# A fused two-layer attention and mixture-of-experts kernel: VectorE's copies first, router rows turned in the projection, unread products in TensorE's waits, one power per row for two norms

## The chip, the cores and the metric

The kernel runs on one core of one Trainium2 chip. Its engines work side by side and meet through semaphores: TensorE (PE, with its weight loads as PEld), VectorE (DVE), ScalarE (ACT), GpSimd (POOL), and the queues of SyncE (SP) and POOL, which issue DMAs. The metric is the device time of one execution in microseconds (us); lower is better. Before the change it is 1354.61 us, the median of 3 runs (1350.93 to 1354.62).

## The reference, cut to what matters

There are four batches of 512 rows with 512 columns each, and a context of 128 columns per row. Four steps follow one another, and each adds to x:

```
x = x + attn0(layernorm(x), ctx)       # q = rms_norm(layernorm(x)), k = rms_norm(ctx), rotary, 16 heads
                                       # over 4 key groups, causal softmax, then @ w_out.T
x = x + ffn0(layernorm(x))             # gate/up/down with 1376 hidden columns, low-rank experts beside it
x = x + attn1(layernorm(x), ctx)       # similarity rows, layer norm over the keys, softmax: added to x
x = x + moe(layernorm(x))              # router of 64 experts, top 8, capacity 128, expert gate/up/down
```

`rms_norm(v) = v * rsqrt(mean(v*v) + 1e-5)`, `layernorm(v) = (v - mean) / sqrt(var + 1e-5)`. So a row of q goes through two norms: with variance v of the row, its scale is `(v + 1e-5)^-0.5 * (v / (v + 1e-5) + 1e-5)^-0.5`.

## The kernel before, in words

All orders are written out by hand, one program per engine. P = 128 rows are a tile, a batch has NT = 4 tiles (t = 0 to 3). The stages are: the start (`front_norms(0)` to `first_group(0)`), `attention(0)`, then for b = 0, 1, 2 the stage `ffn(b)` followed by `attention(b + 1)` with the *tail* of batch b woven into it, then `ffn(3)`, `last_tail(3)` with `last_list`, then 64 experts, and at the end a DMA that adds two halves of the output.

**The start.** VectorE takes statistics of context and x (`bn_stats`, `bn_aggr`, lines 1112 to 1138), GpSimd raises variances to the power -0.5 (`front_power`, line 606). One power takes the context's and x's first norm together; VectorE then works out the second variance (lines 1142 to 1144), and a second power gives the second norm. Line 1246 ends the scale and the shift, step 29 of a chain (`FIRST["scaled"]`); ScalarE's `query_rows` (line 810) waits for it. TensorE waits for all constants (`setup_loaded`) ahead of `first_group(0)`.

**Attention.** G = 4 groups (g) of four heads. For tile t TensorE makes scores (`scores`, six units: two of t = 3, two of t = 2, one of t = 1, one of t = 0), VectorE takes their maximum (`maximum(g, i)`, line 1344), ScalarE the exponentials (`exps`, line 850), TensorE transposes them (`turn`, line 1914), and VectorE or ScalarE copies them out of PSUM (`turned`, line 1353 or 863). The keys and queries of the next group are transposed as `stack` (line 1923) and copied out (lines 1358 and 868); GpSimd prepares them (`stacks`, lines 629 to 640). All transposes go through a ring of three PSUM banks in a written order (`turning_order`), so that each unit waits until the unit three places ahead has been copied out. `times_v(g)` (line 1933) ends a group; it needs all copies of the group. Then `normalise` (line 1377) multiplies by the turned inverse sums (`inverse`, line 1944).

**The tail of batch b, woven into attention(b + 1).** Group 0: x2 and its statistics (`stats_x2`), x2 transposed (`row_T`, line 1997), keys times rows (`keys_out`, line 1962). Group 1: variances and similarity rows (`spread`, `spread_rows`, `similarity`, VectorE's `y` and `peak`). Group 2: softmax's division and x3 (`divide_y`, `x3`, line 1319), statistics of x3 (`stats_x3`). Group 3: aggregation, power, `normed` (line 1274, the router's rows HN), and TensorE's `normed_T` (line 1954, "xT4"), four transposes a tile, in the ring between `turn(3, 2, 3)` and `turn(3, 0)`. Behind group 3 stand the context's transposes (line 2073), the output projection (`projected_out`), and `logits` (line 2005). In attention(0), without a tail, VectorE makes the next queries in two parts (`query_part`, two and three operations) between the copies.

**The last batch.** In `last_tail` nothing else runs beside the tail: similarity rows (line 2321), then VectorE and ScalarE work out x3 and HN, TensorE transposes HN (line 2334) and multiplies by the router (line 2339). `last_list` makes the experts' token lists: positions (line 2109), one-hot products (line 2120), the list itself (line 2157). Then the rows are gathered by DMA and the first expert starts (lines 2359 and 2369).

Of the kernel before, what the change touches and what calls it, by code (L numbers as in the profile page):

```python
# [94 lines left out]
def build(nc, x, ctx_in, w, out, hx, acc):  # L95
# [93 lines left out]
    fvar2, fscale, fms = sb("fvar2", [P, NT]), sb("fscale", [P, NT]), sb("fms", [P, NT])  # L189
# [129 lines left out]
    def bcast(ap, n):  # L319
# [26 lines left out]
    CONSTANTS = [(ident, w["ident"]), (identb, w["identb"]), (mask_qk, w["mask_qk"]),  # L346
                 (wk, w["wk"]), (low_rows, w["low_rows"]),
# [30 lines left out]
    LIST_PAIRS = (4, 8)  # L378
    FRONT_Q = (4, 5, 6, 8)
# [7 lines left out]
    def turning_order(tail):  # L387

        order = []
        for g in range(G):  # L390
# [24 lines left out]
            if tail and g == G - 1:  # L415
                order += [("xT4", 0, "a"), ("xT4", 1, "a")]
# [3 lines left out]
            if tail and g == G - 1:  # L420
                order += [("xT4", 2, "a"), ("xT4", 3, "a")]
# [56 lines left out]
    def ring(a):  # L478

        if a == 0:  # L480
            return Ring(ALONE, (4, 5, 7), 0, 0, 0, 0)
        return Ring(BESIDE, (7, 4, 5), a, len(ALONE) - len(BESIDE) + len(BESIDE) * a,
                    *(turned_by(ALONE, by) - turned_by(BESIDE, by) + turned_by(BESIDE, by) * a for by in "ad"))
# [13 lines left out]
    with nc.Block() as block:  # L497
        @block.sync
        def _(sp):
# [9 lines left out]
            for dst, src, n in ((wq_bc, w["wq"], C), (wkn_bc, w["wkn"], CKV)):  # L509
                sp.dma_start(dst[:, :], bcast(src, n)).then_inc(tables_loaded, 16)  # L510
            for dst, src in CONSTANTS:
                sp.dma_start(dst[(slice(None),) * len(src.shape)], src).then_inc(setup_loaded, 16)
# [85 lines left out]
        def _(pool):  # L598
# [7 lines left out]
            def front_power(fb, n):  # L606

                pool.wait_ge(S["f_in"], 1 + 2 * fb + n)
                if n == 1:
                    ins = pool.tensor_tensor(finv[:, :], fvar[:, :], mhalf[:, :], ALU.pow)  # L610
                else:
                    ins = pool.tensor_tensor(fms[:, :], fvar2[:, :], mhalf[:, 0:NT], ALU.pow)
# [194 lines left out]
        def _(act):  # L807
            def query_rows(t, c0, c1):

                act.activation(X[:, t, c0:c1], XIN[:, t, c0:c1], ACT.Identity, bias=fvar2[:, t:t + 1],  # L810
                               scale=fscale[:, t:t + 1]).then_inc(setup_act, 1)

            def first_stacks():

                act.wait_ge(S["f_dve"], FIRST["scaled"])
                for t in range(NT):
                    query_rows(t, 0, P)
                act.activation(KS[:, :, :].rearrange("p t (r s d) -> p t r s d", r=2, s=2)[:, :, :, 0, :].bitcast(F32R),
# [34 lines left out]
            def attention(a, turns, b):  # L853
# [33 lines left out]

                exps(a, 0, 0)
                exps(a, 0, 1)
                for g in range(G):  # L890
# [13 lines left out]
                    exps(a, g, 4)  # L904
                    if tail and g == 0:
                        normed_T("xT3", 2)
                    if tail and g == 2:
                        exp_y(3)
# [6 lines left out]
                    if tail and g == 3:  # L915
                        normed_T("xT4", 0)
                        normed_T("xT4", 1)
# [5 lines left out]
                    if tail and g == 3:  # L923
                        normed_T("xT4", 2)
                        normed_T("xT4", 3)
# [14 lines left out]
                act.wait_ge(S["o_ready"], 1 + G * (a + 1))  # L940
                act.activation(OTH[:, G - 1, :], OT[:, (G - 1) % 2, :], ACT.Copy).then_inc(S["oT_last_hi"], 1)
# [92 lines left out]
            def last_tail(b):  # L1034
# [10 lines left out]
                for t in range(NT):  # L1045
                    act.wait_ge(S["xT4_ps"], 1 + t + 1)
# [55 lines left out]
        def _(dve):  # L1102
# [9 lines left out]
            def front_norms(fb):  # L1112
# [4 lines left out]
                dve.wait_ge(S["x_loaded"], 16 * (fb + 1))  # L1117
                alone(dve, "dve")
                for i in range(2 * NT):
                    ins = dve.bn_stats(FST6[:, i, :], CTX[:, i, :] if i < NT else XIN[:, i - NT, :])  # L1120
# [5 lines left out]
                for i in range(2 * NT):  # L1126
                    alone(dve, "dve")
                    ins = dve.bn_aggr(FMV[:, i, :], FST6[:, i, :])
                    if i < 2 * NT - 1:
                        ins.then_inc(S["f_dve"], 1)  # L1130
                        fstep.n += 1
                    else:
                        fstep(ins)
                fstep(dve.tensor_tensor(fscale[:, :], FMV[:, 0:NT, 0], FMV[:, 0:NT, 0], ALU.mult))
                fstep(dve.tensor_tensor(fscale[:, :], fscale[:, :], FMV[:, 0:NT, 1], ALU.add))
                fstep(dve.tensor_scalar(fvar[:, 0:NT], fscale[:, :], EPS_RMS, None, ALU.add))
                sig(dve.tensor_scalar(fvar[:, NT:2 * NT], FMV[:, NT:2 * NT, 1], EPS_LN, None, ALU.add),
                    "f_in", 2 * fb + 1)

            def front_scales(fb, meanwhile=lambda: None):  # L1140
                dve.wait_ge(S["f_out"], 1 + 2 * fb + 1)
                fstep(dve.tensor_tensor(fscale[:, :], finv[:, NT:2 * NT], finv[:, NT:2 * NT], ALU.mult))
                fstep(dve.tensor_tensor(fscale[:, :], fscale[:, :], FMV[:, NT:2 * NT, 1], ALU.mult))
                sig(dve.tensor_scalar(fvar2[:, :], fscale[:, :], EPS_RMS, None, ALU.add), "f_in", 2 * fb + 2)
                meanwhile()
                dve.wait_ge(S["f_out"], 1 + 2 * fb + 2)
                fstep(dve.tensor_tensor(fscale[:, :], finv[:, NT:2 * NT], fms[:, :], ALU.mult))
# [96 lines left out]
            dve.wait_ge(tables_loaded, 16 * 6)  # L1244
            front_scales(0, lambda: fstep(first_keys(0, HD, [XN[:, 3, i * P:(i + 1) * P] for i in range(3)])))
            fstep(dve.scalar_tensor_tensor(out=fvar2[:, :], in0=FMV[:, NT:2 * NT, 0], scalar=-1.0, in1=fscale[:, :],
                                           op0=ALU.mult, op1=ALU.mult))
            assert fstep.n == FIRST["scaled"], fstep.n
            dve.wait_ge(setup_act, QUERY_ROWS)
# [77 lines left out]
            def attention(a, turns, b):  # L1327
# [81 lines left out]
                for g in range(G):  # L1409
# [7 lines left out]
                    if rows_in:  # L1417
                        n = stats_x2(b, 3)
# [1086 lines left out]
```

## Time and profile before

| what | us |
|---|---|
| median of 3 runs (lowest, highest) | 1354.61 (1350.93, 1354.62) |
| the profiled execution's own time | 1353.49 |
| its span in the trace | 1351.7 |
| mean granted TensorE clock, as a share of full | 0.957 |
| PE / DVE / ACT / POOL busy | 1199.0 / 746.7 / 525.7 / 447.2 |
| start, up to TensorE's first product | 20.67 |
| attention(0), first to last times_v | 46.35 to 94.97 |
| attention(1), first scores to its last times_v | 235.75 to 322.67 |
| last tail and list, up to the first expert's product | 929.24 to 997.87 |

The trace is of one execution. The engine table says how long each engine was busy; the chain of waits says who released whom on the way to the end; a table of stretches gives busy time and granted clock by stage. A granted clock of 1.00 is 2.4 GHz and 0.50 is 1.2 GHz.

### The profile page before, as it was taken

Reading aid. Unit: us, or ns where it says so; the run is one execution under the profiler, and the core shown is the slowest. Engines: PE = TensorE matmul, PEld = TensorE weight load, DVE = VectorE, ACT = ScalarE, POOL = GpSimd, SP = SyncE. Lnnn points to the kernel's source line nnn. Section 1 sums busy time; section 2 is a strip of 40 time slices with the busy share of each in tenths; the row PEclk is TensorE's granted clock in tenths of the full one; section 3 lists DMA queues with packets and bytes.
Section 4 is the critical chain, followed back from the end, with each engine's and each line's share of the span. In section 5 each row is a group of like instructions: output and inputs, shape, how many; then the busy total and the mean of one; then the engine's idle time right before and its main releaser. Section 6 shows DMA issues by size and latency. Waiting matters only on the chain.

```text
span 1351.7 us, 19376 instructions
## 1 busy us (share of the span) xinstructions
PE 1199.0 (89%) x6494; PEld 877.1 (65%) x6494; DVE 746.7 (55%) x1509; ACT 525.7 (39%) x1186; POOL 447.2 (33%) x506
## 2 busy tenths in 40 slices
PE   2789999888999988899999899998469999999990
PEld 2567787666777766777866677775346666666650
DVE  6866665785688678578866847563622222222220
ACT  4774222775412377442246643221223233333320
POOL 0531334321133532113443202121035655555530
PEclk9999999989999998999999899999569999999995
DMA  8012320001233000213300013624439999999847
GB/s 281 1 60 90 117 97 33 1 32 65 104 132 111 19 1 32 104 70 127 129 1 1 32 65 117 251 98 184 178 111 332 347 362 352 357 344 352 246 54 140
DMA packets 45745, 186.98 MB, mean 138 GB/s; under 512 B 6556, under 2 KB 9628, under 8 KB 31204
## 3 DMA queue, kind: packets, MB, share of 16 engines
q1 hardware_dynamic: 30804, 146.13, 28.3%
q0 software_dynamic: 14864, 39.85, 12.9%
q8 instruction: 44, 0.72, 0.2%
q14 instruction: 33, 0.27, 0.1%
HBM read 155.26 MB, written 34.90 MB: 141 GB/s over the span
## 4 chain that ended last, share of the span: by engine, by line
PE 71%; DVE 15%; ACT 4%; issue 3%; DMA 3%; POOL 2%; DVEq 0%; POOLq 0%; SPq 0%; ACTq 0%
PE PS L2369 13%; PE PS L1832 10%; PE PS L1834 9%; PE PS L1833 9%; PE PS L2385 4%; PE PS L1914 3%; PE PS L2389 3%; PE PS L1933 3%; DVE NM L1344 2%; PE PS L1851 2%; PE PS L2359 2%; ACT P L850 2%; DMA WRAW<-in_ffn 1%; DVE PT L1353 1%; PE PS L2202 1%
## 5 line engine op out<-in xcount | busy, mean ns | idle before, releaser
L2369 PE MATMUL PS<-WE,XGT 128*128 128x384 f32 x512 | 194.8, 504 | 1.5 <-DVE HM L1809 0.8
L850 ACT ACTIVATE P<-PS,NM 128x512 f32<-128x512 f32 (+3 forms) x256 | 132.0, 533 | 39.0 <-DVE NM L1344 38.6
L689 POOL CAST HH<-HID 128x512 fp32r<-128x512 f32 x44 | 37.2, 846 | 324.9 <-DVE HID L1697 320.6
L1832 PE MATMUL PS<-XTH,WHI 128*128 128x512 f32 x352 | 141.3, 401 | 3.4 <-DVE WLO L1640 3.4
L969 ACT ACTIVATE WHI<-WRAW 128x1280 fp32r<-128x1280 f32 x44 | 56.0, 1274 | 217.9 <-DMA WRAW<-in_ffn 217.9
L1834 PE MATMUL PS<-XTH,WLO 128*128 128x512 f32 x352 | 138.2, 393 | 0.0
L1833 PE MATMUL PS<-XTL,WHI 128*128 128x512 f32 x352 | 138.1, 392 | 0.0
L2369 PEld LDWEIGHTS PS<-WE,XGT 128*128 128x128 f32 x512 | 88.3, 192 | 57.7 <-issue 23.4
L1914 PE MATMUL PS<-ident,P 128*128 128x128 f32 x640 | 98.7, 291 | 28.2 <-ACT P L850 6.2
L1816 DVE COPY HMT<-PS 128x256 f32<-128x256 f32 x64 | 27.2, 425 | 163.7 <-PE PS L2378 163.7
L1344 DVE TENSOR_REDUCE NM<-PS 128x2 f32<-128x1024 f32 (+2 forms) x96 | 98.7, 1039 | 27.7 <-PE PS L1841 27.4
L1914 PEld LDWEIGHTS PS<-ident,P 128*128 128x128 f32 x640 | 74.9, 149 | 41.1 <-ACT P L850 19.9
L662 POOL TENSOR_TENSOR sm<-sm,mhalf 128x4 f32<-128x4 f32 (+1 forms) x20 | 17.7, 884 | 213.3 <-DVE sm L1263 187.4
L764 POOL DMA_INDIRECT XG<-hx,IDX x64 | 64.6, 1010 | 50.8 <-POOL IDX L761 39.8
L1078 ACT ACTIVATE SL<-PS 128x192 f32<-128x192 f32 x64 | 21.1, 330 | 154.6 <-PE PS L2369 154.6
L1832 PEld LDWEIGHTS PS<-XTH,WHI 128*128 128x128 f32 x352 | 66.3, 188 | 20.3 <-DVE WLO L1640 6.2
L1834 PEld LDWEIGHTS PS<-XTH,WLO 128*128 128x128 f32 x352 | 66.3, 188 | 16.1
L1833 PEld LDWEIGHTS PS<-XTL,WHI 128*128 128x128 f32 x352 | 66.3, 188 | 14.1
L1353 DVE COPY PT<-PS 128x512 f32<-128x512 f32 (+1 forms) x96 | 61.4, 639 | 16.7 <-PE PS L1914 16.6
L1851 PE MATMUL PS<-KST,QST 128*128 128x512 f32 (+3 forms) x256 | 67.0, 366 | 2.7 <-ACT P L850 2.2
L776 POOL DMA_INDIRECT out<-YE,IDX x32 | 51.0, 1593 | 53.4 <-ACT YE L1084 36.5
L2385 PE MATMUL PS<-WE,HMT 128*128 128x256 f32 x256 | 66.0, 381 | 0.5 <-DVE HMT L1816 0.5
(312 smaller groups left out, 2702.2 us busy)
## 6 DMA issues: line engine op xcount, KB each, us to landing
WE<-in_we SPq DMA_DIRECT2D x64, 1152.0 KB, 8.0
WRAW<-in_ffn SPq DMA_DIRECT2D x44, 1060.0 KB, 4.9
acc<-HN SPq DMA_DIRECT2D x17, 256.0 KB, 6.0
XIN<-in_x SPq DMA_DIRECT2D x4, 1024.0 KB, 5.8
out<-X SPq DMA_DIRECT2D x4, 1024.0 KB, 4.2
out<-acc POOLq DMA_DIRECT2D x1, 4096.0 KB, 22.9
hx<-HN SPq DMA_DIRECT2D x3, 1152.0 KB, 4.5
CTX<-in_ctx SPq DMA_DIRECT2D x4, 256.0 KB, 2.8
```

Source lines behind the costliest of these rows:

```text
L764: pool.indirect_dma_start(out=XG[s][:, :], out_offset=None, in_=hx, in_offset=bass.IndirectOffsetOnAxis(ap=IDX1[s][:, 0:1], axis=0),).then ...
L850: act.activation(prob(t, n), PS[:, c0:c0 + (t + 1) * P], ACT.Exp, bias=NM[:, c:c + 1], accum_out=SSUM[:, c:c + 1]).then_inc(S["p_ready"], 1)
L969: act.activation(WHI[slot][:, 0:WD], WRAW[slot][:, 0:WD], ACT.Copy).then_inc(S["wg_hi"], 1)
L1344: dve.tensor_reduce(NM[:, t * HPG + n0:t * HPG + n0 + nh], src, AX, ALU.max, negate=True).then_inc(S["s_max"], 1)
L1353: dve.tensor_copy(prob_T(t, n0, nh), src).then_inc(S["ring_d"], 1)
L1832: pe.matmul(dst, a[0], b_[0], start=first, stop=False, **kw)
L1833: pe.matmul(dst, a[0], b_[1], start=False, stop=False, **kw)
L1834: return pe.matmul(dst, a[1], b_[0], start=False, stop=last, **kw)
L1851: pe.matmul(PS[:, a:a + n_keys], QST[n0 + n][:, t * P:(t + 1) * P], KST[:, 0:n_keys], start=(a % 512 == 0), stop=False, skip_group_check=True)
L1914: mm = pe.transpose(bank(bk, c, c + P), prob(t, n0 + n)[:, j * P:(j + 1) * P], ident[:, :])
L2369: mm = pe.matmul(bank(2 + s % 2, 0, 2 * F1), XGT[s % 2][:, k, :], WE[s][:, k * 2 * F1:(k + 1) * 2 * F1], start=(k == 0), stop=(k == KC - 1))
L2385: pe.matmul(bank(5 + h, 0, CH), HMT[s % 2][:, 0, :], WE[s][:, EDOWN + h * CH:EDOWN + (h + 1) * CH], start=True, stop=False)
```

## The change

There are five edits.

1. *VectorE's copies first.* In the woven attention VectorE's tail work moves behind `maximum` and `turned`; in attention(0) each `query_part` moves behind a copy. Instructions stay the same. ScalarE copies `xT3` tile 2 out ahead of `exps(4)`.
2. *Router rows turned in the projection.* `normed_T` leaves the ring; its four tiles are transposed between the parts of `projected_out`, into banks 6, 7, 1, 6, and ScalarE copies them out there, with semaphores of their own. The context's transposes move ahead of `times_v(3)`. The ring starts at another bank.
3. *Unread products.* `keep_clock(bank, n)` issues n products of 512 columns (bf16) into a bank that nobody reads: 10 at the start, 54 ahead of the transposes of HN in the last tail, 14 and 18 in `last_list`, 22 behind it.
4. *One power for both norms.* x's scale becomes `(v * (1 + 1e-5) + 1e-10)^-0.5`, one power of 4 columns; the context's power is a second one of 4 columns. The statistics of the context no longer wait for x.
5. *Loads.* ident, identb and mask_qk count towards `tables_loaded`; TensorE waits at the start for that only, and for `setup_loaded` ahead of the first projection.

```
+    ROWS_BANK = (6, 7, 1, 6)
-        return Ring(BESIDE, (7, 4, 5), a, ...
+        return Ring(BESIDE, (4, 5, 7), a, ...
 # front_norms: x waited for only at i == NT; x's aggregation first
+                        sig(dve.tensor_scalar(fvar[:, NT:2 * NT], FMV[:, NT:2 * NT, 1], 1.0 + EPS_RMS,
+                                              EPS_LN * EPS_RMS, ALU.mult, ALU.add), "f_in", 2 * fb + 1)
-                fstep(dve.tensor_tensor(fscale[:, :], finv[:, NT:2 * NT], finv[:, NT:2 * NT], ALU.mult))
-                fstep(dve.tensor_tensor(fscale[:, :], fscale[:, :], FMV[:, NT:2 * NT, 1], ALU.mult))
-                sig(dve.tensor_scalar(fvar2[:, :], fscale[:, :], EPS_RMS, None, ALU.add), "f_in", 2 * fb + 2)
 # VectorE, one group g of attention after the change (tail work in brackets, by group)
     maximum(g, 2); turned(g, 3, 0); query_part(1, 1) if g == 0
     [1: weighted] [2: y(3)]
     maximum(g, 3); turned(g, 3, 2)
     [2: peak(3)] [1: similarity_variances] [3: stats_x3(1)]
     normalise(g - 1); maximum(g, 4); turned(g, 2, 0)
     [1: similarity_scales, y(0)]
     maximum(g, 5); stack(g + 1, 1)
     [0: stats_x2(3)] [1: peak(0)]
     turned(g, 2, 2); query_part(g + 2, 0)
     [0: stats_x2(0)] [1: y(1)] [2: divide_y(0, 2), x3(0)] [3: stats_x3(2)]
     stack(g + 1, 3); turned(g, 1, 0, 2)
     [0: stats_x2(1)] [1: peak(1)] [2: x3(1)]
     divisors(g)
     [3: stats_x3(3), aggregate, variances]
     turned(g, 0, 0, 4)
     [3: normed, all four tiles]
     maximum(g + 1, 0); maximum(g + 1, 1); query_part(g + 2, 1)
     [0: stats_x2(2), aggregate, variances] [1: y(2), peak(2)]
     [2: divide_y(2, 4), x3(2), x3(3), stats_x3(0)]
 # TensorE
+            def keep_clock(bk, n):
+                for _ in range(n):
+                    pe.matmul(bank(bk).rearrange("p (r k) -> p r k", k=P), identb[:, :],
+                              mask_qk[:, :].unsqueeze(1).broadcast_to([P, NT, P]), start=True, stop=True)
+                    if g == G - 1:
+                        context_T()
                     times_v(g)
                 for t in range(NT - 1):
                     if t == 1:
                         inverse(G - 1)
                     projected_out(t, 0, KC - 1)
+                    if tail and t < 2:
+                        normed_T(2 * t)
+                        normed_T(2 * t + 1)
 # ScalarE, behind group 3: unload(3); xT4 tiles 0, 1; output_high(); xT4 tiles 2, 3
```

## Rows read from the trace of the kernel before

**Rows 1.** Page: busy us (share) xinstructions; chain of waits by engine; one costly group.
```profile
PE 1199.0 (89%) x6494; PEld 877.1 (65%) x6494; DVE 746.7 (55%) x1509; ACT 525.7 (39%) x1186; POOL 447.2 (33%) x506
...
PE 71%; DVE 15%; ACT 4%; issue 3%; DMA 3%; POOL 2%; DVEq 0%; POOLq 0%; SPq 0%; ACTq 0%
...
L2369 PE MATMUL PS<-WE,XGT 128*128 128x384 f32 x512 | 194.8, 504 | 1.5 <-DVE HM L1809 0.8
```

**Rows 2.** Stretches, one per attention group: length, PE PEld DVE ACT POOL busy, clock, DMA.
```profile
46.35:63.68 17.33, 14.45 (x125) 10.49 (x124) 14.93 (x23) 13.62 (x42) 7.48 (x13) 1.00 0.00 1
63.68:79.38 15.70, 14.29 (x126) 10.53 (x124) 12.11 (x18) 13.82 (x42) 8.55 (x11) 1.00 0.01 1
79.38:92.68 13.30, 11.00 (x97) 7.62 (x96) 10.24 (x15) 11.97 (x39) 6.46 (x3) 1.00 0.00 1
235.70:257.06 21.36, 17.48 (x124) 13.25 (x122) 17.15 (x30) 16.65 (x46) 7.86 (x14) 1.00 0.00 1
257.06:280.45 23.39, 21.64 (x150) 14.25 (x148) 16.75 (x28) 15.30 (x47) 9.69 (x16) 1.00 0.00 1
280.45:301.19 20.74, 17.40 (x126) 13.42 (x125) 18.07 (x29) 14.29 (x45) 5.52 (x7) 0.84 0.14 51
301.19:320.37 19.18, 14.40 (x113) 10.85 (x112) 14.24 (x26) 13.73 (x42) 2.84 (x3) 0.91 0.01 1
```

**Rows 3.** Chain of waits, then instructions in time, at the start: start us, us, what.
```profile
7.28 3.26 DVE FST L1120 x8
...
10.68 1.07 DVE L1128 BATCH_NORM_AGGREGATE FMV<-FST 128x2 f32<-128x6 f32 x8 [0.15 <-DVE FST L1120]
12.64 1.68 POOL L610 TENSOR_TENSOR finv<-fvar,mhalf 128x8 f32<-128x8 f32 x1 [12.21 <-DVE fvar L1137]
15.05 0.29 DVE L1200 TENSOR_TENSOR XN<-CTX,finv 128x128 f32<-128x128 f32 x1
17.02 1.65 ACT L810 ACTIVATE X<-XIN,fvar,fscale 128x128 f32<-128x128 f32 x4 [15.00 <-DVE fvar L1246]
20.67 1.08 PE L1868 MATMUL PS<-ident,KS 128*128 128x128 f32 x4 [20.67 <-DVE KS L1232]
```

**Rows 4.** Instructions in time in attention(0), with the idle time before them.
```profile
43.83 0.40 POOL L629 CAST KS<-KR 128x256 fp32r<-128x256 f32 x1 [2.94 <-DVE QR L1226]
54.46 0.60 PE L1923 MATMUL PS<-ident,KS 128*128 128x128 f32 x4
61.88 0.63 PE L1914 MATMUL PS<-ident,P 128*128 128x128 f32 x4 [1.49 <-DVE PT L1353]
92.68 2.36 PE L1933 MATMUL PS<-PT,CTX 128*32 128x512 f32 x32 [0.83 <-issue]
```

**Rows 5.** The same in attention(1).
```profile
245.63 0.63 PE L1997 MATMUL PS<-ident,X 128*128 128x128 f32 x4 [2.18 <-DVE PT L1353]
288.77 1.77 DVE L1319 SCALAR_TENSOR_TENSOR X<-XN,sm,X 128x512 f32<-128x512 f32 x2
292.28 1.09 PE L1923 MATMUL PS<-ident,QS 128*128 128x128 f32 x4 [1.85 <-DVE PT L1353]
```

**Rows 6.** A stretch of the last tail, columns as in rows 2.
```profile
947.50:958.00 10.50, 0.00 (x0) 0.00 (x0) 8.60 (x20) 2.33 (x6) 1.01 (x1) 0.50 0.92 372
```

**Rows 7.** TensorE's instructions in time: two of attention(1), then the last tail.
```profile
248.29 0.39 PE L1841 MATMUL PS<-mask_qk,identb 128*128 128x512 bf16 x1
336.05 3.68 PE L2005 MATMUL PS<-rw,XTF 128*128 128x64 f32 x32
...
958.42 3.67 PE L2334 MATMUL PS<-ident,HN 128*128 128x128 f32 x16 [14.19 <-DVE HN L1274]
961.89 6.93 PE L2339 MATMUL PS<-rw,XTF 128*128 128x64 f32 x32
986.54 3.65 PE L2157 MATMUL PS<-OWN,SPREAD 128*128 128x64 f32 x16 [1.20 <-DVE OWN L1589]
997.87 4.90 PE L2369 MATMUL PS<-WE,XGT 128*128 128x384 f32 x8 [0.73 <-issue]
```

More of the change, by code:

```diff
@@ L939, in attention @@
                 unload(G - 1)
-                act.wait_ge(S["o_ready"], 1 + G * (a + 1))
-                act.activation(OTH[:, G - 1, :], OT[:, (G - 1) % 2, :], ACT.Copy).then_inc(S["oT_last_hi"], 1)
+                if tail:
+                    for t in range(NT):
+                        act.wait_ge(S["xT4_ps"], 1 + NT * b + t + 1)
+                        act.activation(XTF[:, :, t * P:(t + 1) * P], bank(ROWS_BANK[t]).rearrange(
+                            "p (k q) -> p k q", k=KC), ACT.Copy).then_inc(S["xT4_sb"], 1)
+                        if t == 1:
+                            output_high()
+                else:
+                    output_high()
             def softmax_exp(b):
@@ L1859, in ranks_out, with keep_clock @@
                       skip_group_check=True).then_inc(S["ffn_ps"], 1)
+            def keep_clock(bk, n):
+                for _ in range(n):
+                    pe.matmul(bank(bk).rearrange("p (r k) -> p r k", k=P), identb[:, :],
+                              mask_qk[:, :].unsqueeze(1).broadcast_to([P, NT, P]), start=True, stop=True)
             def first_group(fb):
@@ L2000, in logits @@
                 def logits():
[L2002 removed]
+                    pe.wait_ge(S["xT4_sb"], 1 + NT * (b + 1))
                     for t in range(NT):
@@ L2007, in logits, with context_T @@
                     mm.then_inc(S["lgt_ps"], 1)
+                def context_T():
+                    for t in range(NT):
+                        mm = pe.transpose(bank(0, t * P, (t + 1) * P), CTX[:, t, :], ident[:, :])
+                    mm.then_inc(S["ctxT_ps"], 1)
                 for g in range(G):
@@ L2053, in attention @@
                     turn(g, 1, 2, 2)
-                    if tail and g == G - 1:
-                        normed_T("xT4", "xn4_ready", HN, 2)
-                        normed_T("xT4", "xn4_ready", HN, 3)
                     if g < G - 1:
@@ L2069, in attention @@
                         keys_out()
-                if tail:
-                    turns.out(pe, "xT4", NT - 1)
-                for t in range(NT):
-                    mm = pe.transpose(bank(0, t * P, (t + 1) * P), CTX[:, t, :], ident[:, :])
-                mm.then_inc(S["ctxT_ps"], 1)
                 def projected_out(t, k0, k1):
@@ L2089, in attention @@
                     projected_out(t, 0, KC - 1)
+                    if tail and t < 2:
+                        normed_T(2 * t)
+                        normed_T(2 * t + 1)
                 pe.wait_ge(S["ctxT_sb"], 1 + a + 1)
```

218 lines of the change are left out of this document (110 added, 108 removed).

## The prediction

> **What bounds the kernel now.** I read the page first: TensorE is busy for 1199.0 of 1351.7 us, and it holds 71% of the chain that ended last, VectorE 15% [rows 1]. So time can be won only where TensorE waits or runs at a low clock. The table of stretches says where that is. In the groups of attention(1) TensorE is busy for 17.48 of 21.36, 21.64 of 23.39, 17.40 of 20.74 and 14.40 of 19.18 us, and in the last two the mean granted clock is 0.84 and 0.91, which means 1.2 GHz for about 6.6 and 3.5 us (share below 1.00, doubled, times the length) [rows 2]. Attention(2) and (3) repeat these stretches within 0.1 us from group 1 on. Third, the instructions in time name what TensorE waits for: VectorE's copies. Fourth, the last tail: 14.19 us without a product, and 1.2 GHz from then on until the first expert [rows 6, 7]. The feed-forward stages (TensorE busy throughout) and the 64 experts are not touched, so whatever comes earlier ahead of them moves the end by as much.
>
> **The start (one power, loads).** Before, eight statistics take 3.26 us from 7.28 on, behind x's arrival [rows 3]. The context's four are a quarter as wide; the x rows take about 0.6 us each, so x's end at about 9.75. Half of the eight aggregations (1.07) is 0.54, one variance operation 0.2: GpSimd starts at 10.7. Its power took 1.68 for 8 columns [rows 3]; for 4 I take 1.1, which lies between nothing and 1.68. One shift operation later, at 12.1, ScalarE may scale rows; before it was 17.02: 4.9 us earlier. The keys need the second power too: it starts at 12.0 (context's aggregation and three operations stand ahead), ends at 13.1, and the key work, begun at 15.05 before, begins at 13.2, now all of it ahead of the query's first operations. Keys 1.6, first query 1.3, low part 0.4: TensorE's first transposes at about 16.5 instead of 20.67 [rows 3]. I take 4.1 (bounds: 1.8, what the keys' start moves by, and 4.9). The wait for tables costs nothing if they land by 13 us; they are about 2 MB, and what was loaded up to then is more. The 10 unread products end before 16.5 even at twice 0.39 each. The first four transposes took 1.08 against 0.60 later [rows 3, 4], so the start runs slowly; I count nothing for that.
>
> **Attention(0), copies first.** In groups 0 and 1 the query's three operations stand ahead of the copy that TensorE waits for: 1.49 us in each (one of the two is shown) [rows 4]. Group 2, without them, takes 15.70 against group 1's 17.33 [rows 2]. That is 1.5 us twice, 3.0. GpSimd gets the queries about 5 us later (it started at 43.83 [rows 4], for some 6.5 us of stacks), while TensorE asks for their first stack at 54.46 [rows 4]; moved 1.5 earlier that is 53.0, and the stack is ready by about 51. So nothing is lost; without that cover it would be the 5 us. The context's transposes (0.44) fall into the 0.83 us in which TensorE waits ahead of the last times_v [rows 4]: 0.4. Sum 3.4 (bounds 0 and 3.7).
>
> **Attention(1) to (3), copies first and rows moved.** I walked each group through its ring.
> Group 0: `row_T(1)` waited 2.18 us for a copy that stood behind three statistics [rows 5]. With maximum and copy first that copy is 1.7 us earlier; ScalarE's early copy of tile 2 saves as much again in part, and the statistics fill VectorE's waits. Of the 3.9 us not busy [rows 2] I take 2.1. Group 0's last statistics and the aggregation (1.2 us) stand ahead of GpSimd's power and so of its stacks, which start some 5 us later; TensorE has `keys_out` (3.2 us) and a third of a group ahead of them, so nothing.
> Group 1: 1.75 us not busy; `y(0)` ahead of `maximum(5)` and the copy ahead of `peak(1)` remove two waits of 0.86 and 0.56: 1.3.
> Group 2: two x3 (1.77) and a reciprocal stand ahead of `maximum(4)`, and TensorE stands still for 1.85 until the copy, then runs its transposes at half rate (four in 1.09) [rows 5]. After the change VectorE is about 1.9 us earlier at `maximum(4)` and 2.5 at `maximum(5)`; then ScalarE (exponentials, `exp_y(3)` ahead of the stack's copy) is late next, and TensorE waits for it for about 1.8 us instead of 1.0. Of 3.3 us not busy and 3.3 lost to the clock I take 2.8.
> Group 3: attention(0)'s group 3, without a tail, takes 13.30 [rows 2]. The tail's remains: VectorE enters 1.3 us late from x3 and statistics behind group 2, and the last statistic with aggregation (1.2) stands ahead of the last copy. 13.3 + 1.3 + 1.2 = 15.8, against 19.18: 3.3 (bounds: 0 and 5.9).
> The projection grows by 16 transposes at 0.11 each (32 small products take 3.68 [rows 7]): 1.8, less 0.4 for the context's, which move into the wait ahead of times_v: 1.3 in the order of the engines, since TensorE has no gap there. ScalarE's copies are done 1 us before TensorE asks for the context's.
> Sum: 2.1 + 1.3 + 2.8 + 3.3 - 1.3 = 8.2 a batch, 24.6 for three (bounds -1.3 and 13 a batch).
>
> **The last tail.** 54 products follow line 2321 at about 944. The nearest row has one at 0.39 with its latency [rows 7]; behind one another I take 0.23, the spacing of the 512-column products of the same trace: 12.4 us, inside the gap of 14.19. (Price of one between 0.2 and 0.39; at 0.39 they would end 7 us late.) Then the clock should be up at 958.4. Transposes and logits took 3.67 and 6.9; at full rate 1.9 (VectorE paces HN) and 3.7 as in attention(1) [rows 7]: 5.1 saved. The 14 and 18 products (3.2 and 4.1) stand in waits of 4.8 and 5.0 us less one fold product: nothing. The one-hot products are few per us, so whether the clock holds until line 2157 (3.65, half of it to win) is even: 1.2 with the last one-hots. The 22 behind it take 5.1 in a wait of 5.8; if at half rate at first they are up to 2 us late, and then the first expert's 8 products cost 3.0 (194.8/512 each [rows 1]) instead of 4.90. I take 1.2 net. Sum 7.5 (bounds -8, if all run at half rate, and 10.5).
>
> The Trainium skill ("TensorE: Matmul & The Clock Gate", Part 4: PE-mode transpose) says that transposes don't count as busy for the clock. That speaks against the 5.1 above, since 16 transposes follow the 54 products; the 16 and the 32 logits here ran wholly at half rate [rows 7], which agrees. By it the tail would gain 3 rather than 7.5.
>
> **Sum.** 4.1 + 3.4 + 24.6 + 7.5 = 39.6. The profiled execution took 1353.5, so 1313.9; the median of the runs is 1.1 above that execution: 1315.
>
> **Rivals.**
> (a) *ScalarE takes VectorE's place.* It is busy for 60 us of 84.7 in the four groups of attention(1), 16.65 of 21.36 in group 0 [rows 2], and its order hardly changes. Then TensorE's idle time is renamed and the clock still falls in groups 2 and 3: 4 us a batch instead of 8.2, and 2 less elsewhere: 39.6 - 12.6 - 2 = 25, so 1330. For it: both stalls of group 2 end near a ScalarE copy. Against it: the largest waits end with VectorE's copies.
> (b) *The clock is down at HN.* Between the last of 54 and the first transpose 2 us stay open; a wait of 1.85 was enough for half rate at 292.28 [rows 5]. Logits stay slow, later products run at half rate, the tail gains 3: 1319.5.
> (c) *The moved work is paid in full.* What VectorE did inside a group now stands right ahead of `maximum(g+1, 2)` and of the last copy: 1.2 behind group 0, 2.1 behind group 2, 1.2 in group 3, with the projection 1.3, that is 5.8 a batch, 17.4, and 1.45 twice in attention(0), while the earlier copies win nothing. Less 4.1 and 7.5 that is 8.7 slower: 1363. It decides if VectorE's idle time ahead of that maximum (1.2 us in attention(0), as in group 3) is shorter than the moved work and TensorE waits for exponentials anyway. Against it: the wait of 2.18 at 245.63 [rows 5].
> (d) *The slow clock in the products themselves*, 108 of them at twice 0.23 against 28 us of waits: 20 us late in the tail, with the rest as forecast 1342.
>
> **How the numbers follow.** Forecast 0.54, (b) 0.18, (a) 0.18, (d) 0.04, (c) 0.04, no change 0.02. The forecast's own range is 1303 to 1327. 8 in 10 reach from 1302 to 1335, which takes in (a) and (b) and leaves (c) and (d) out. A measurement of this kernel tells 0.3% (4 us) from nothing. Faster 0.94, the same 0.02, slower 0.04.
>
> **What would show it.** TensorE's first transposes at 16.5; group 2 of attention(1) near 18 us with a clock of 0.95 or more, group 3 near 16; the projection's first part 1.3 longer; 54 products ending ahead of HN; logits in 3.7 us. The forecast is wrong if the groups stay above 20 and 18 us, if TensorE waits for ScalarE's exponentials for as long as it did for copies, if a product of 512 columns costs near 0.39, or if logits still take 6.9.

## The result, and the profile after

The changed kernel takes **1322.37 us**, median of four runs (1322.07 to 1322.65), beside 1353.69 for the kernel before on the same chip: ratio **0.977**, 95% interval 0.975 to 0.979, a gain of 31.3 us. I had said 1315, with 1302 to 1335 as the range: the sign held, and so did the mechanism in the groups and at the start; the size was 7 to 8 us too large. A second session gave 1322.28 for the same kernel. All medians here are of fast executions; one of e8's six took 2425.51 us and is not counted. The profiled execution took 1322.24 us with a span of 1320.4 (before: 1353.49 and 1351.7).

The page: busy us of each engine, then the chain of waits by engine, then a costly group.

```profile
PE 1214.4 (92%) x6612; PEld 874.8 (66%) x6612; DVE 744.1 (56%) x1493; ACT 525.3 (40%) x1186; POOL 442.0 (33%) x506
...
PE 71%; DVE 14%; ACT 6%; issue 3%; DMA 2%; POOL 2%; DVEq 0%; SPq 0%; POOLq 0%; ACTq 0%
...
L2388 PE MATMUL PS<-WE,XGT 128*128 128x384 f32 x512 | 192.7, 499 | 1.5 <-DVE HM L1813 0.8
```

Against [rows 1] TensorE is busy for 15.4 us more in a span that is 31.3 shorter (the 118 unread products alone are 29.8 us of it, the rest is shorter by 14.4); VectorE's share of the chain fell by a point and ScalarE's rose by two. The stretches, from one times_v to the next (columns as in [rows 2]): attention(0) groups 1 to 3, attention(1) groups 0 to 3 and from times_v(3) to the logits; then the stretch to the logits in attention(2) and in attention(3).

```profile
40.59:56.43 15.84, 14.29 (x125) 10.48 (x123) 15.30 (x23) 13.79 (x42) 7.70 (x12) 1.00 0.00 1
56.43:72.34 15.91, 14.20 (x125) 10.52 (x124) 13.68 (x21) 14.18 (x42) 10.48 (x14) 1.00 0.00 1
72.34:85.93 13.59, 11.51 (x99) 8.22 (x100) 10.59 (x15) 11.71 (x39) 6.47 (x3) 1.00 0.01 2
228.52:248.17 19.65, 17.39 (x123) 13.22 (x122) 15.61 (x24) 16.45 (x46) 5.43 (x10) 1.00 0.01 1
248.17:271.06 22.89, 22.05 (x148) 14.39 (x148) 18.19 (x33) 15.25 (x46) 11.44 (x18) 1.00 0.01 1
271.06:288.83 17.77, 15.02 (x126) 10.87 (x126) 15.02 (x25) 14.29 (x45) 5.29 (x9) 1.00 0.01 1
288.83:304.64 15.81, 12.31 (x100) 8.91 (x100) 14.74 (x27) 11.42 (x38) 0.75 (x1) 0.92 0.18 68
304.64:323.69 19.05, 19.05 (x107) 13.57 (x107) 8.44 (x16) 6.80 (x13) 2.80 (x4) 0.89 0.30 115
...
531.42:549.71 18.29, 18.29 (x106) 13.26 (x107) 8.40 (x16) 6.80 (x13) 2.79 (x4) 0.92 0.32 120
...
757.46:774.45 16.99, 16.99 (x106) 13.08 (x107) 8.45 (x16) 6.80 (x13) 2.81 (x4) 1.00 0.33 129
```

Group 2 fell from 20.74 to 17.77 and its clock rose from 0.84 to 1.00; group 3 from 19.18 to 15.81. But the same instructions from times_v(3) to the logits take 19.05, 18.29 and 16.99 us, and the clock column says why: 0.89, 0.92, 1.00. Before they took 15.68 in all three, without the 16 transposes of the rows. TensorE's instructions in time show the place, and the tail:

```profile
16.36 1.11 PE L1878 MATMUL PS<-ident,KS 128*128 128x128 f32 x4 [2.24 <-DVE KS L1235]
...
302.26 1.09 PE L1924 MATMUL PS<-ident,P 128*128 128x128 f32 x4 [1.22 <-ACT PT L863]
303.14 1.06 PE L2025 MATMUL PS<-ident,CTX 128*128 128x128 f32 x4
304.64 4.44 PE L1943 MATMUL PS<-PT,CTX 128*32 128x512 f32 x32 [0.44 <-issue]
...
918.45 11.82 PE L1868 MATMUL PS<-mask_qk,identb 128*128 128x512 bf16 x54
932.81 3.07 PE L2352 MATMUL PS<-ident,HN 128*128 128x128 f32 x16 [2.54 <-DVE HN L1280]
935.67 4.29 PE L2357 MATMUL PS<-rw,XTF 128*128 128x64 f32 x32
...
958.04 3.65 PE L2173 MATMUL PS<-OWN,SPREAD 128*128 128x64 f32 x16 [1.20 <-DVE OWN L1593]
961.48 6.29 PE L1868 MATMUL PS<-mask_qk,identb 128*128 128x512 bf16 x22
...
968.93 2.82 PE L2388 MATMUL PS<-WE,XGT 128*128 128x384 f32 x8 [0.73 <-issue]
```

times_v(3) takes 4.44 us instead of 2.36: it runs at 1.2 GHz for nearly all of it. In the tail the spread (OWN, SPREAD) is still at half rate, the first expert's eight products no longer (2.82 against 4.90 in [rows 7]). Last, TensorE's waits in total (us, times, longest):

```profile
PE PS L1924 <- ACT KST L868: 11.7, 9, 1.7
...
PE PS L1924 <- ACT PT L863: 7.2, 10, 1.2
PE PS L1924 <- ACT P L850: 6.2, 13, 0.8
```

The waits for VectorE's copies, up to 2.18 us each in [rows 5], are 0.4 us at most now; the large ones that are left inside attention end with ScalarE.

### The profile page after: what moved, and what is told of

Same layout as the page of the kernel before. It is cut to its first block, busy times and chain, and to the rows that moved or that the text cites. A ratio compares the mean times of both kernels' runs of the same rounds, so it can differ in the third digit from the quotient of the medians.

```text
span 1320.4 us, 19584 instructions
## 1 busy us (share of the span) xinstructions
PE 1214.4 (92%) x6612; PEld 874.8 (66%) x6612; DVE 744.1 (56%) x1493; ACT 525.3 (40%) x1186; POOL 442.0 (33%) x506
## 4 chain that ended last, share of the span: by engine, by line
PE 71%; DVE 14%; ACT 6%; issue 3%; DMA 2%; POOL 2%; DVEq 0%; SPq 0%; POOLq 0%; ACTq 0%
PE PS L2388 13%; PE PS L1836 10%; PE PS L1838 9%; PE PS L1837 9%; PE PS L2404 4%; ACT P L850 4%; PE PS L2408 3%; PE PS L1924 3%; DVE NM L1350 3%; PE PS L1943 2%; PE PS L2378 2%; PE PS L1855 2%; DMA WRAW<-in_ffn 2%; PE PS L2219 1%; PE PS L2218 1%
## 5 line engine op out<-in xcount | busy, mean ns | idle before, releaser
L1924 PE MATMUL PS<-ident,P 128*128 128x128 f32 x640 | 94.5, 280 | 25.8 <-ACT KST L868 11.7
L1924 PEld LDWEIGHTS PS<-ident,P 128*128 128x128 f32 x640 | 69.9, 142 | 40.3 <-ACT P L850 24.6
L692 POOL TENSOR_TENSOR HL<-HID,HH 128x512 fp32r<-128x512 f32 x44 | 64.6, 1468 | 3.5
## 6 DMA issues: line engine op xcount, KB each, us to landing
out<-acc POOLq DMA_DIRECT2D x1, 4096.0 KB, 22.9
```

Of the source, the lines that this page charges most:

```text
L692: pool.tensor_tensor(HL[slot][:, :], HID[:, :], HH[slot][:, :], ALU.subtract).then_inc(S["hl_ready"], 1)
L1924: mm = pe.transpose(bank(bk, c, c + P), prob(t, n0 + n)[:, j * P:(j + 1) * P], ident[:, :])
```

## The experiments

Each was timed beside the kernel before, whose median was 1353.79 us for e1 to e4, 1354.19 for e5 to e8, 1354.12 for e9 and e10, and 1354.26 for e11 and e12; these are four sessions on four chips. A kernel's own runs lie 0.6 to 6 us apart, so differences between kernels are good to 1 or 2 us (e7 has a single run). Where I give a place, it is read in the one profiled execution, in the same stretches as above.

**e1: VectorE's order of before** (and ScalarE's), all else as changed; for one group-2 stretch:

```
-                    turned(g, 3, 2)
...
                     if soft:
                         peak(3)
+                    turned(g, 3, 2)
...
+                    if soft:
+                        divide_y(b, 0, 2)
+                        x3(0)
+                        x3(1)
                     maximum(g, 4)
```

> The changed kernel with VectorE's (and ScalarE's) order of the kernel before in all groups; the rows stay turned in the projection. Theory (VectorE's order set TensorE's waits, and what is missing from my forecast was lost to the clock behind group 3): the groups lengthen by 3.0 us in attention(0) and by 1.7 + 0.5 + 3.0 in groups 0 to 2 of each later batch; group 3 by about 1.2, since its normed rows are early but no longer turned in it; the projection's first part falls back from 19.05, 18.29 and 16.99 to about 17.0 in all three, because the last copy is early and the clock holds: -3.7. Sum 3.0 + 15.6 + 3.6 - 3.7 = 18.5, so 1341 us. Rival (ScalarE took VectorE's place, the order itself is worth little): 1326 to 1330 us, with groups 0 to 2 within 1 us of the changed kernel's.

Measured 1343.8 us, ratio to before 0.993 (0.991 to 0.994), 21.4 above the changed kernel. Attention(1): 21.29, 23.39, 20.63, 16.12. TensorE waits for VectorE's copies again:

```profile
PE PS L2012 <- DVE PT L1359: 6.5, 3, 2.2
PE PS L1935 <- DVE PT L1359: 6.4, 6, 1.9
PE PS L1926 <- DVE PT L1359: 6.1, 8, 1.5
```

So the order is two thirds of the gain, and ScalarE had not simply taken VectorE's place. One part of my theory fell: the stretch to the logits took 17.74, 18.35 and 18.17, with times_v(3) at 3.15 to 3.76 us, though the last copy is early here. So the clock falls behind group 3 without a late copy too.

**e2: group 3 as before** (rows turned inside it, the context's transposes behind times_v):

```
+            if tail and g == G - 1:
+                order += [("xT4", 0, "a"), ("xT4", 1, "a")]
...
-                    if tail and t < 2:
-                        normed_T(2 * t)
-                        normed_T(2 * t + 1)
```

> The changed kernel with group 3 of attention(1) to (3) as before: the normed rows made early and turned inside the group, the context's transposes behind times_v; groups 0 to 2 keep the new order. Theory: group 3 takes 19.2 to 19.5 us again instead of 15.8, the stretch from its times_v to the logits 15.7 instead of 19.05, 18.29, 16.99; net +0.2, +0.9, +2.2 us, 3.3 in all: 1326 us. Rival (moving the rows costs as much as it gives, with the clock it drops): 1322 us or less.

1329.4 us, 0.982 (0.981 to 0.984): 7.0 above the changed kernel, where I had expected 3.3. Group 3 takes 20.50, 20.85 and 20.79, the stretch behind it 15.6 each time. Moving the rows pays about 5 us a batch in the group and costs 1.4 (clock up) to 3.5 (clock down) behind it. But this group 3 is not quite that of the kernel before (19.18, 19.13, 19.06): three statistics of x3 stand ahead of `maximum(3)`, where before there were two, and more of x3's work comes late from group 2. So 1.3 to 1.7 of the 5 us come from joining new and old orders, and not from the rows; against the kernel before, group 3 of the changed kernel gained 3.3.

**e3: no unread products.** `for _ in range(0 * n)` in `keep_clock`.

> The changed kernel without any of its 118 unread products (10 at the start, 54, 14, 18 and 22 in the last tail). Theory: the tail loses what it gained, 5.4 us (the logits take 6.9 us again, the one-hots and the spread 3.65 at half rate, the first expert's products 4.9 instead of 2.8); the 10 at the start ran at half rate themselves and brought nothing (0 to 0.2): 1328 us. Rival (the products delay HN's transposes and the gather by as much as the clock gives): 1322 us within 1. If the 10 products do warm the start, TensorE's first score comes more than 0.3 us later.

1326.2 us, 0.979 (0.978 to 0.980): 3.9 above the changed kernel, where I had expected 5.6. The loss is not where I had put it. TensorE's instructions in the tail, then stretches of it:

```profile
934.19 3.68 PE L2352 MATMUL PS<-ident,HN 128*128 128x128 f32 x16 [14.19 <-DVE HN L1280]
937.65 3.84 PE L2357 MATMUL PS<-rw,XTF 128*128 128x64 f32 x32
...
970.88 5.12 PE L2388 MATMUL PS<-WE,XGT 128*128 128x384 f32 x8 [0.73 <-issue]
```

```profile
936.00:938.00 2.00, 2.00 (x12) 2.00 (x10) 0.00 (x0) 1.29 (x3) 0.00 (x0) 0.51 0.75 284
938.00:940.00 2.00, 2.00 (x20) 2.00 (x19) 0.00 (x0) 0.50 (x1) 0.00 (x0) 1.00 0.69 249
```

The logits take 3.84 us with 14.19 us of silence before them and no product: the clock rose at the end of the 16 transposes. Their end is 1.53 later than in the changed kernel, of which 1.38 was there at the last logits of attention(3): between these two profiles the 54 products bought 0.15. The first expert's eight (5.12 against 2.82) are 2.3 of the rest; from the last logits of attention(3) on, the tail is 2.9 longer without products. The 1.38 ahead of it is mostly the clock again, lower in other stretches of attention than in the changed kernel's profile. What the 54 are worth in the mean is not shown: in the eleven profiles with bf16 products ahead of HN (the changed kernel, e1, e2, e4 to e6, e8 to e12) the logits took 3.68 to 4.33, in the two with nothing there 6.93 (before) and 3.84. The 10 at the start didn't bring the first scores earlier (22.12 here, 22.16 in the changed kernel). From the first transposes to the first times_v it takes 24.43 here, 24.23 in the changed kernel's profile and 23.40 in e5's, so no gain of theirs can be told from the way the clock varies there.

**e4: two powers at the start**, as before.

> The changed kernel with the norms of the start in two powers as before (x awaited ahead of all statistics, scale of a row from two inverse roots), the loads in the new order. Theory: the first transposes come at about 20.5 us instead of 16.36, and everything behind them is later by that: 1326.5 us. Rival (the gain came from waiting for fewer tables): 1323 us, first transposes at 17.

1326.8 us, 0.979 (0.977 to 0.981). First transposes at 20.57, the first scores of attention(1) 4.34 later: theory. (0.24 of it is x's arrival: the statistics began at 7.29 us, in the changed kernel at 7.05.)

**e5: the changed kernel again.**

> The changed kernel once more, as control for the runs beside it: 1322.4 us, within 0.3%. The stretch from times_v(3) to the logits took 19.05, 18.29 and 16.99 us in its first profile and other values between 17.0 and 19.05 in three kernels that leave these instructions alone. If that is the clock falling at a moment that varies from run to run, the same kernel shows other values here, with every other stretch within 0.1 us.

1322.3 us, 0.977 (0.975 to 0.978). From times_v(3) to the logits, in the three batches:

```profile
304.93:323.60 18.67, 18.67 (x107) 13.67 (x107) 8.44 (x16) 6.79 (x13) 2.79 (x4) 0.91 0.30 117
531.33:548.33 17.00, 17.00 (x106) 13.09 (x107) 8.43 (x16) 6.79 (x13) 2.79 (x4) 1.00 0.34 130
756.01:774.44 18.43, 18.43 (x106) 13.33 (x107) 8.41 (x16) 6.79 (x13) 2.79 (x4) 0.92 0.31 119
```

The same program, other batches hit (19.05, 18.29, 16.99 the first time), and group 2 of attention(1) at 19.09 instead of 17.77, which the expectation had ruled out. A fall of the clock there costs 1.3 to 2.1 us and is not tied to one batch; the sum over the three is 54.3 and 54.1, so the median hardly shows it.

**e6: more products**, in group 3's waits and in the tail:

```
+                    if g == G - 1:
+                        keep_clock(3, 2)
                     turn(g, 2, 3)
...
+                    keep_clock(0, 4)          # behind each one-hot group
...
-                keep_clock(7, 54)
+                keep_clock(7, 64)
```

> The changed kernel with more unread products: 2, 1, 5 and 2 in group 3's waits of 0.59, 0.26, 1.22 and 0.44 us (all four attentions), 64 instead of 54 ahead of HN, 4 behind each of the four one-hot groups. Theory (the clock that falls behind group 3 falls for want of products): the clock holds, times_v(3) takes 2.36 and the stretch to the logits 17.0 in all three, 3.4 less in sum; the gap of 2.54 ahead of HN closes, the last one-hots take 0.64 and the spread 1.8 instead of 3.65, 2.3 less: 1317 us. Rival (idle time inside group 3 is not what drops it, or the products hold up the turns): 17.7 to 19 us stay in the projection, and group 3 grows by 1 us: 1323 us.

1316.4 us, 0.972 (0.971 to 0.974), 5.9 below the control. Group 3 and the stretch behind it in attention(1), that stretch in attention(2) and (3), and group 2 of attention(3); then the tail:

```profile
289.30:304.75 15.45, 13.52 (x111) 8.88 (x110) 14.38 (x27) 11.49 (x38) 0.74 (x1) 1.00 0.19 69
304.75:321.74 16.99, 16.99 (x106) 13.09 (x107) 8.42 (x16) 6.79 (x13) 2.80 (x4) 1.00 0.33 129
529.37:546.35 16.98, 16.98 (x106) 13.08 (x107) 8.45 (x16) 6.79 (x13) 2.79 (x4) 1.00 0.34 129
755.22:772.23 17.01, 17.01 (x106) 13.07 (x107) 8.44 (x16) 6.79 (x13) 2.79 (x4) 1.00 0.34 129
720.60:739.76 19.16, 16.41 (x127) 12.50 (x126) 15.46 (x25) 14.40 (x45) 5.29 (x9) 0.91 0.00 1
```

```profile
930.45 2.02 PE L2360 MATMUL PS<-ident,HN 128*128 128x128 f32 x16 [0.37 <-DVE HN L1280]
932.31 3.68 PE L2365 MATMUL PS<-rw,XTF 128*128 128x64 f32 x32
...
953.69 1.97 PE L2181 MATMUL PS<-OWN,SPREAD 128*128 128x64 f32 x16 [0.35 <-DVE OWN L1593]
...
962.92 4.51 PE L2396 MATMUL PS<-WE,XGT 128*128 128x384 f32 x8 [0.73 <-issue]
```

With its idle time filled the clock holds behind group 3 in all three. It holds there in e10, e11 and e12 too, which have the same 10 products: 12 stretches of 12. In the eight kernels with the rows in the projection and no products in group 3 (the changed kernel, e1, e3, e4, e5, e7, e8, e9) it held in 8 of 24. The 10 products cost nothing: group 3 of attention(2) took 15.80, in the changed kernel 15.79. But the clock fell in group 2 instead, in attention(1) and (3): 19.05 and 19.16 for 17.77. No products stand there; why it fell twice here and once or not at all in the others isn't shown. The spread runs at full rate. The 22 products now end 1.12 us ahead of the gather, and the first expert is at half rate again; in e10 and e11 they end 1.03 and 1.08 ahead of it and the same eight products took 2.82, so the gap alone doesn't decide it.

**e7: transposes for the 54 products.**

```
-                keep_clock(7, 54)
+                for _ in range(108):
+                    pe.transpose(bank(7, 0, P), ident[:, :], ident[:, :])
```

> The changed kernel with the 54 unread products ahead of HN replaced by 108 transposes of 128 columns of float32. At full rate they take as long (0.11 each, 11.9 us). If transposes count for the clock as products do, it stays at 1.00 through them and they end before HN. If they don't, as the rule that I weighed says, the granted clock falls to 0.50 some us after 918, they take up to 24 us and hold up HN's turns by about 10 us: 1332 us. A profile tells; no timing.

One run, 1324.5 us; span 1321.8. The 108 took 11.95 us. The granted clock while they run, and after the gap of 2.40 us behind them:

```profile
918.00:920.00 2.00, 2.00 (x20) 2.00 (x19) 2.00 (x4) 0.81 (x2) 0.00 (x0) 1.00 1.01 429
...
926.00:928.00 2.00, 2.00 (x21) 2.00 (x20) 1.90 (x5) 0.00 (x0) 0.00 (x0) 1.00 0.92 387
...
932.00:934.00 2.00, 2.00 (x13) 1.99 (x11) 0.41 (x1) 1.59 (x4) 0.00 (x0) 0.55 0.30 115
```

Ten microseconds of nothing but transposes at 2.4 GHz: while they run, they hold the clock as products do. It fell only behind the gap, as in the changed kernel, but for longer: here the logits ran at half rate to their end, 6.93 us, and in no profile with products in this place did they take over 4.33. One profile doesn't tell whether that is the transposes or chance.

**e8: ScalarE's order.**

```
-                    exps(a, g, 4)
...
+                    exps(a, g, 4, 0, 2)
                     if g < G - 1:
                         stack(g + 1, 0, KST)
-                    exps(a, g, 5)
+                    exps(a, g, 4, 2, 4)
                     turned(g, 2, 3)
...
                         stack(g + 1, 2, QST[1])
+                    exps(a, g, 5)
```

> The changed kernel with another order on ScalarE in every group: the keys' stack copy between the second and third exponential of unit 4, the copy turned(2,3) and the stack copy 2 ahead of unit 5's exponentials, exp_y(3) behind them. Theory (ScalarE's place in the ring is what TensorE now waits for: 11.7 us on the stack copy, 7.2 on its turned copy): the waits of 1.04 and 0.39 in each of 12 groups go and about 0.3 comes back ahead of the last turn; 0.8 to 1.1 a group in attention(0), less where VectorE is next (groups 0 and 1 of the others): 8 to 12 us, 1312 us. Rival (VectorE or the exponentials themselves are as late): 1320 us, the wait renamed.

1318.4 us, 0.973 (0.972 to 0.975): 3.9 below the control, less than a half of what I expected. Groups of attention(1): 18.83, 23.75, 16.66, 15.38. Attention(0) did not move (15.86, 15.89); the wait has another name there:

```profile
54.16 0.63 PE L1934 MATMUL PS<-ident,QS 128*128 128x128 f32 x4 [1.32 <-DVE QST L1365]
```

VectorE's copy of stack 3 stands behind a query operation. Group 1 grew from 22.89 to 23.75: there exp_y(0) stands ahead of the copy of stack 4, and unit 5's exponentials now stand ahead of both; the next scores stood still for 0.47 us, where in the changed kernel they had not waited.

**e9: VectorE's last copy earlier.**

```
-                    divisors(g)
-                    if norm: ... stats_x3(b, 3), aggregate(), variances(b, 5)
                     turned(g, 0, 0, 4)
+                    divisors(g)
+                    if norm: ... the same
```

`query_part(g + 2, 0)` and `stats_x2(b, 0)` move too, from behind `turned(g, 2, 2)` to behind `turned(g, 1, 0, 2)`.

> The changed kernel with three more moves in VectorE's order: the last copy turned(g,0,0,4) ahead of the divisors in every group; in group 3 the last statistic, the aggregation and the variances behind it too; in attention(0) the query's first operation, and in group 0 the second statistic, behind the copies of stack 3 and of turned(1,0,2). Theory (the tail's work ahead of the last copy is 1.2 us of my 15.8 for group 3, and the divisors 0.6): times_v(3) of attention(1) to (3) starts 1.5 earlier, attention(0)'s groups 0.5 each; 1.5 x 3 + 1.5 = 6 less: 1316 us, and the clock holds behind group 3 more often. Rival (TensorE gets the copy earlier but waits for ScalarE's or for the exponentials): 1321 us.

1332.1 us, 0.983 (0.982 to 0.985): 10 slower than the changed kernel, where I had expected 6 less. times_v(3) did come 0.65 us earlier, with its 2.36 us, but the stretch behind it took 21.29 in all three batches, of which TensorE waited 2.63 and had the clock at 0.92. TensorE's first product of the projection:

```profile
311.01 0.50 PE L1834 MATMUL PS<-woH,OTH 128*128 128x512 f32 x1 [2.63 <-POOL OTL L675]
```

GpSimd splits group 2's output behind the power that waits for these variances: a wait in the order of a third engine, which had been covered. Attention(0)'s groups took 16.72, 16.64 (15.84, 15.91 before the moves). I put that down to the divisors, which behind the copy hold up the next group's maxima; e10, which has the same moves beside ScalarE's new order and takes 15.51 and 15.52, speaks against it, so the cause is open.

**e10: all together**: e6 + e8 (with exp_y(0) behind group 1's copies and exp_y(1) in group 2) + e9.

> All of it together: the new order of ScalarE, with exp_y(0) and exp_y(1) behind the copies of group 1 and in group 2; VectorE's three moves; 10 products in group 3's waits, 64 ahead of HN, 4 behind each one-hot group. Each alone gave or should give 4, 6 and 6 us against the changed kernel. Theory (ScalarE and VectorE each hide what the other would give, so together they give more than the sum in attention(0), where ScalarE's order alone brought nothing because VectorE's copy of stack 3 stood behind a query operation): 1302 to 1306 us. Rival (the exponentials bound the groups): the sum without interaction, or less, 1308 us or more. If the 10 products now stand in waits that are gone, group 3 is up to 1 us longer than without them.

1315.3 us, 0.972 (0.971 to 0.974), where I had expected 1302 to 1306. Attention(1) 18.82, 23.21, 16.79, 14.44, but 19.67 behind it: the same GpSimd, in time order:

```profile
302.65 1.01 POOL L661 TENSOR_TENSOR sm<-sm,mhalf 128x4 f32<-128x4 f32 x1 [22.71 <-DVE sm L1270]
...
304.40 1.26 POOL L675 TENSOR_TENSOR OTL<-OT,OTH 128x512 fp32r<-128x512 f32 x1 [0.18 <-POOL OTH L672]
...
305.72 0.50 PE L1835 MATMUL PS<-woH,OTH 128*128 128x512 f32 x1 [2.64 <-POOL OTL L675]
```

The same wait stands in e9 and here, but with e6's products ahead of it the clock held. The stretch behind group 3 of attention(1), first in e9, then in e10; the other two batches are alike in each:

```profile
306.01:327.30 21.29, 18.66 (x107) 14.42 (x108) 10.03 (x24) 6.90 (x13) 3.54 (x4) 0.92 0.27 103
```

```profile
300.72:320.39 19.67, 17.03 (x108) 13.08 (x108) 10.04 (x24) 6.80 (x13) 3.53 (x4) 1.00 0.29 111
```

**e11: mended.**

```
# to e10
-                power(b, 5)
                 split_output(a, 2)
+                power(b, 5)
...
+                    if g < G - 1:
+                        divisors(g)
                     turned(g, 0, 0, 4)
...
```

> As the kernel before it (all together), with two mends. GpSimd splits the output of group 2 ahead of the power for norm 5, not behind it: in both kernels with the last copy moved, TensorE waited 2.6 us for that split at the start of the projection, since GpSimd stood at the power whose variances come later now; the stretch from times_v(3) to the logits was 19.67 and 21.29. And the divisors are ahead of the last copy again in groups 0 to 2: behind it they held up the next group's maxima, and with them the exponentials. Theory: that stretch returns to 17.0 (-2.7 three times), group 1 to 22.4 to 22.9 (-0.3 to -0.8), attention(0) within 0.3: 1305.5 us. Rival (something else holds the projection, HN's turns for example, because the variances are 1 us later): 19 us stay, 1313 us.

**1307.5 us, 0.966 (0.964 to 0.968)**: the fastest, 14.8 below the control of e5 and 46.8 below the kernel before. Behind group 3: 16.94, 16.94, 16.96. Attention(1): 19.34, 23.10, 16.78, 13.98; attention(0) 15.51, 16.25, 13.51. GpSimd's order gave 2.7 us in each of three batches, as expected, and that is the whole difference: the divisors' move gave nothing (the four groups of attention(1) sum to 73.2 here and to 73.3 in e10, the three of attention(0) to 45.3 and 45.2), and group 1, which I had put at 22.4 to 22.9, stayed.

**e12: the next query wholly behind the maxima.**

```
                     turned(g, 1, 0, 2)
-                    query_part(g + 2, 0)
...
+                    query_part(g + 2, 0)
                     query_part(g + 2, 1)
```

> As the mended kernel, and in attention(0) both parts of the next query stand behind the next group's first two maxima, none between the copies. Theory (VectorE is busy for 15.1 of 15.5 us of such a group, so its sum decides and not its order): attention(0) within 0.3 us of the kernel beside it, the wait of 0.73 ahead of the third scores gone and back at the third maximum: same time within 0.5 us. Rival (the exponentials start 1.3 us earlier and carry it through): 1.3 us in two groups, 2.6 less.

1308.7 us, 0.967 (0.965 to 0.969); e11's interval covers it. Attention(0)'s groups 15.97 and 17.22 against 15.51 and 16.25: 1.4 worse, neither theory. The later maximum shows as a wait ahead of a turn, where e11 waited for 0.17:

```profile
62.36 0.63 PE L1926 MATMUL PS<-ident,P 128*128 128x128 f32 x4 [1.43 <-ACT P L850]
```

## Why the prediction was right, and where it was not

**The start, 4.1.** Measured 4.31 (20.67 to 16.36), of which 0.23 is x's arrival (statistics from 7.28 and from 7.05 us); e4 alone gives 4.2. GpSimd's power of four columns took 1.05 (I took 1.1) and started at 10.52 (10.7). The 10 products ran at half rate, 4.45 us in all; no gain of theirs shows.

**Attention(0), 3.4.** Before the first scores of attention(1) it had won 7.23 with the start, so 2.9. Group 1 fell by 1.49, as sized. Groups 2 and 3 grew by 0.2 and 0.3 (15.70 to 15.91, 13.30 to 13.59), which I had not counted.

**Attention(1) to (3), 24.6.** Group 0: 1.7 for my 2.1. Group 1: 0.5 for 1.3, and this is a term I mis-sized: TensorE was to be idle for 0.45 us there; it is for 0.84, and is busy for 0.4 more. Group 2: 3.0 for 2.8, with the clock at 1.00. Group 3: 3.4 for 3.3. Together 8.6 for 9.5. The projection: the moved rows cost 1.3 where the clock holds (16.99 against 15.68), as worked out; but I had counted it at full rate in all three, and it cost 3.4, 2.6 and 1.3. The step that was mis-sized most is "The projection grows ... 1.3": it cost 7.3 in three batches for my 3.9, so 3.4 us of the missing 8 are the clock behind group 3. e5 shows that it comes and goes in one and the same program, e6 that filling group 3's waits ends it there. What the batches gave in all is 5.1, 6.0 and 7.2, that is 18.3 for 24.6.

**The last tail, 7.5.** 5.5 measured, from attention(3)'s logits to the end of the first expert's eight products. The largest piece, 5.1 for transposes and logits at full rate (by its own terms 5.0), came to 3.2 (7.36 us for 10.60), and it isn't shown that the 54 products brought it: e3 has its logits in 3.84 without a product, so before's 6.93 was one outcome of at least two. That this piece came out with the right sign is in part luck. Rival (b) happened in part as well: behind the gap of 2.54 the clock fell, for some 3 us. Yet e2 has the same 54 products and the same gap of 2.54, and its clock held. Two microseconds of each behind the gap, first the changed kernel, then e2:

```profile
934.00:936.00 2.00, 2.00 (x12) 2.00 (x10) 0.12 (x1) 1.38 (x4) 0.00 (x0) 0.50 0.43 164
```

```profile
944.00:946.00 2.00, 2.00 (x21) 1.89 (x18) 1.01 (x3) 1.61 (x4) 0.00 (x0) 1.00 0.13 46
```

What the products did buy lies at the end, 2.3 us in the first expert. The 22 behind the spread were about 0.1 us late (VectorE read the gathered rows at 967.48, TensorE began at 967.60), which I had allowed 2 for.

**The rule that I weighed.** The granted clock was 1.00 through 108 transposes in e7, and in e3 it rose from 0.50 after 3.5 us of nothing but transposes (the logits had just begun). In the kernel before it did not rise in 10.4 us of the same transposes and logits. The Trainium skill ("TensorE: Matmul & The Clock Gate", Part 4: PE-mode transpose) says that transposes don't count as busy; both traces go against it for these float32 transposes, and the measurement decides. What is left for the rule is e7's slow logits behind the gap. By the rule I had priced the tail at 3 instead of 7.5; the 5.5 measured lies between, for another reason.

**The rivals.** (a) was partly true: TensorE's waits are ScalarE's now (11.7, 7.2 and 6.2 us), yet groups 2 and 3 kept their gain. e8 shows that ScalarE's order was worth 4. (c) was refuted by e1: the order of before costs 21 us. (d) too: one of the 54 products took 0.22. The measured 1322.4 lies nearer to (b)'s 1319.5 than to my 1315, but not by (b)'s mechanism: 6 of the missing 8 us are in attention(1) to (3), only 2 in the tail.

**Slips in the working.** Group 2 of the kernel before repeats within 0.2 us (20.74, 20.84, 20.93), not 0.1.

**Left open.** Why the clock falls behind group 3 (and in group 2: once each in e2 and e5, twice in e6) in some batches and not in others with the same instructions within 0.1 us, and why half-rate logits lasted 6.93 us in the kernel before and e7 and not in e3. No row here tells.

## What to carry to other kernels

When one engine's order is changed, list what every other engine has queued behind the values that come later: e9 gave TensorE its copy earlier and lost 10 us, 7.9 of them in waits for GpSimd; e11, with that order swapped, took 2.7 us off each batch. Two engines that feed one ring can hide each other's lateness: in group 3 of attention(1) ScalarE's order alone gave 0.4 us (e8), VectorE's alone 0.65 (e9), both together 1.8 (e11). Elsewhere no such sum shows, and no run has VectorE's moves with GpSimd's mend alone. Short waits ahead of a long busy stretch are worth filling: 10 unread products in waits of 0.26 to 1.22 us kept the clock up behind group 3 in 12 stretches of 12, against 8 of 24 without them. A gain in a stretch that ran at 1.2 GHz should be priced at both levels and read from more than one profile, since a single trace shows one outcome.

## What the runs showed of the hardware

- Transposes of 128 float32 columns, 0.11 us each, held the granted clock at 1.00 for 10 us (e7).
- A gap of 2.4 to 2.5 us in front of HN was followed by 1.2 GHz in the changed kernel and e7, but not in e2 (2.54 us, clock 1.00); a gap of 0.37 (e6) was not either.
- The same work at half rate can stay there: 16 transposes and 32 small products ran 10.4 us without a pause at 0.50 in the kernel before; in e3 the clock rose after 3.5 us of them.
- The clock column can mislead at the very start: the 10 products took 4.45 us in all, twice the 0.22 each of the 54, while it read 1.00.
- x's arrival moves the start from run to run: its statistics began at 7.05 us in the changed kernel's profile and at 8.99 in e11's, with the same loads in the same order; all behind it moved by as much (first transposes 16.36 and 18.29).
